# Six of eight input-weight pieces of a selective-scan layer made inside the attention before it, and the layer's opening steps interleaved

## The reference, cut to what matters

```python
proj = einsum('bld,pd->blp', hidden, in_proj_w)
gate, hbc, dt = proj[..., :I], proj[..., I:I+CONV_DIM], proj[..., -H:]
conv = conv_bias + sum_k pad(hbc)[:, k:k+L, :] * conv_weight[:, k]     # K = 4
x, B, C = split(silu(conv))
dt_p = softplus(dt + dt_bias);  A = -exp(A_log);  dA = exp(dt_p * A)
state = state * dA_t + (dt_p * x)_t * B_t;  y_t = state . C_t          # scan over tokens
y = rmsnorm_per_group(y + x * D) * norm_weight * silu(gate)
out = einsum('bli,di->bld', y, out_proj_w)
```

## Time and profile before

| | us |
|---|---|
| median of 3 runs | 4329.69 (4328.75 to 4337.84) |
| the profiled execution, its own time | 4338.59 |
| span of the profile | 4336.8 |
| PE busy | 3790.7 (87%) |
| DVE busy | 2798.5 (65%) |
| ACT busy | 2281.6 (53%) |
| POOL busy | 1887.1 (44%) |
| mean granted TensorE clock | 0.924 |

### The profile page before, as it was taken

The page is one execution under the profiler, slowest core; times in us unless marked ns, Lnnn a source line. Parts: engine busy times, 40 slices in busy tenths (PEclk is TensorE's granted clock), DMA queues, the critical chain, the costliest instruction groups (busy, mean ns, idle before and its releaser), DMA issues.

```text
span 4336.8 us, 63426 instructions
## 1 busy us (share of the span) xinstructions
PE 3790.7 (87%) x21648; PEld 1878.8 (43%) x21648; DVE 2798.5 (65%) x4529; ACT 2281.6 (53%) x3945; POOL 1887.1 (44%) x1566
## 2 busy tenths in 40 slices
PE   6799996889889858999999999999999984867899
PEld 2344442322332225555555555555555552443344
DVE  6522223675567357888888888888888866566322
ACT  5422222455445537667666766667666753453222
POOL 5400000000000217778787877778787774553000
PEclk7699996889888979999999999999999997898999
DMA  3100002000100010000000000000000001012100
GB/s 109 46 1 0 0 0 50 16 1 16 18 1 1 1 57 12 19 17 7 30 1 25 12 24 13 19 18 7 30 1 24 6 25 37 23 45 62 40 10 19
DMA packets 62763, 91.20 MB, mean 21 GB/s; under 512 B 12310, under 2 KB 36393, under 8 KB 62453
## 3 DMA queue, kind: packets, MB, share of 16 engines
q1 hardware_dynamic: 62456, 87.31, 7.2%
HBM read 73.62 MB, written 6.85 MB: 19 GB/s over the span
## 4 chain that ended last, share of the span: by engine, by line
PE 65%; DVE 15%; issue 8%; ACT 6%; POOL 3%; DMA 2%; SPq 1%; DVEq 0%; POOLq 0%; ACTq 0%
PE psum L332 14%; PE psum L333 14%; PE psum L334 14%; PE psum L1373 3%; DVE arena L1522 3%; PE psum L2434 2%; PE psum L2430 2%; PE psum L2422 2%; PE psum L1346 2%; PE psum L2391 2%; PE psum L1357 2%; PE psum L2413 1%; ACT xn L218 1%; PE psum L1342 1%; DVE x L2119 1%
## 5 line engine op out<-in xcount | busy, mean ns | idle before, releaser
L332 PE MATMUL psum<-xt_hi,arena 128*128 128x512 f16 (+1 forms) x2272 | 875.9, 386 | 48.4 <-DVE arena L1512 14.5
L333 PE MATMUL psum<-xt_lo,arena 128*128 128x512 f16 (+1 forms) x2272 | 874.3, 385 | 0.0
L334 PE MATMUL psum<-xt_hi,arena 128*128 128x512 f16 (+1 forms) x2272 | 871.9, 384 | 0.0
L2217 POOL TENSOR_TENSOR arena<-arena 128x1024 f16<-128x1024 f16 x256 | 514.3, 2028 | 79.8 <-DVE arena L2029 48.4
L1291 POOL TENSOR_TENSOR rs<-sd,epsc 128x1 f32<-128x1 f32 x15 | 8.2, 550 | 1153.5 <-DVE sd L1566 1153.5
L1522 DVE TENSOR_REDUCE arena<-psum 128x1 f32<-128x512 f32 (+3 forms) x608 | 365.1, 655 | 176.3 <-PE psum L1346 174.9
L332 PE MATMUL psum<-arena 128*128 128x512 f16 (+1 forms) x1152 | 422.2, 370 | 59.4 <-DVE arena L2842 20.5
L1474 ACT ACTIVATE arena<-psum 128x512 f32<-128x512 f32 x576 | 319.9, 598 | 276.9 <-PE psum L1357 181.4
L333 PE MATMUL psum<-arena 128*128 128x512 f16 (+1 forms) x1152 | 422.2, 370 | 0.0
L334 PE MATMUL psum<-arena 128*128 128x512 f16 (+1 forms) x1152 | 421.7, 370 | 0.0
L332 PEld LDWEIGHTS psum<-xt_hi,arena 128*128 128x128 f16 x2272 | 225.1, 99 | 301.0 <-issue 18.6
(11 more groups left out here) (330 smaller groups left out, 7834.7 us busy)
## 6 DMA issues: line engine op xcount, KB each, us to landing
arena<-m_wi SPq DMA_DIRECT2D x64, 320.0 KB, 3.0
arena<-m_wo SPq DMA_DIRECT2D x32, 256.0 KB, 2.6
arena<-arena SPq DMA_DIRECT2D x96, 64.0 KB, 2.5
x<-L_attn_x SPq DMA_DIRECT2D x4, 1024.0 KB, 8.8
out<-x SPq DMA_DIRECT2D x4, 1024.0 KB, 4.3
arena<-gate_wT SPq DMA_DIRECT2D x16, 224.0 KB, 2.6
arena<-up_wT SPq DMA_DIRECT2D x16, 224.0 KB, 2.5
arena<-down_wT SPq DMA_DIRECT2D x14, 256.0 KB, 2.6
```

The source lines that it names most:

```text
L332: nc.tensor.matmul(out, lh, rh, start=start, stop=False)
L333: nc.tensor.matmul(out, lh, rl, start=False, stop=False)
L334: return nc.tensor.matmul(out, ll, rh, start=False, stop=stop)
L2217: nc.gpsimd.tensor_tensor(m4_ar[:, q], heads[q].broadcast_to([P, HG, P]), m4_le.unsqueeze(1).broadcast_to([P, HG, P]), ALU.mult).then_inc( ...
```

## The change

Six of the eight pieces move into L1 attention: at the first unit of p = 10 to 15, ACT and DVE each make one, and SP fetches it at row p (a "piece" step each). The pieces are taken in the order 1, 2, 3, 5, 6, 7, and all six pass through the first half of m4_raw; 0 and 4, whose target overlaps L1's masks, are made after feed-forward steps 13 and 14, and the dt weights after step 15. SP fetches those two and the small parameters once the attention's last transposes are done, not after the feed-forward. L1's feed-forward weights move to other addresses, are fetched at row 11 and not 2, and split at p = 13 and not 5.

In the opening of L2 attention the 8 KB memset of m4_acc shrinks to its last tile; group 0 writes m4_acc by `tensor_scalar` instead of adding to it. Both dt products run at once, in two banks (7 and 3). The projections 0 to 3, their `before` and their convolutions are laid between the links of the two step-size chains; 4 to 9 follow. ACT waits for x_kept ahead of the first Abs.

```diff
@@ steps2
-                    if p == 5 and i == 0:
+                    if p == 13 and i == 0:
                         steps.append(("ffn_weights", 0))
+                    if p >= EARLY4 and i == 0:
+                        steps.append(("piece", p - EARLY4))
...
                 steps.append(("ffn", n))
+                if n in (LAST3 + 1, LAST3 + 2):
+                    steps.append(("piece", NT - EARLY4 + n - LAST3 - 1))
+                if n == LAST3 + 3:
+                    steps.append(("dt_weights", 0))
...
+        EARLY4 = NT - 6
@@ sp_l1_attn
                 elif what == "row":
-                    if p == 2:
+                    if p >= EARLY4:
+                        if p > EARLY4:
+                            sp.wait_ge(m4_wlo, p - EARLY4 + 2)
+                        sp_piece(sp, p - EARLY4)
+                    if p == 11:
+                        sp.wait_ge(a2_md, AT2["qp", 1, 1, KT - 1] + 3)
+                        sp.wait_ge(a2_dma, 16 * 2 * QDMA)
                         sp.dma_start(s3_raw, ...).then_inc(s3_in, 16)
@@ sp_l2_attn
+        FIRST4 = (1, 2, 3, 5, 6, 7, 0, 4)
...
-            arena_free(sp, 4)
+            sp.wait_ge(a2_at, 2 * NT)
+            sp.wait_ge(m4_wlo, 6 + 2)
+            for i in (6, 7):
+                sp_piece(sp, i)
...
-            for q in range(2):
-                fetch(q, wi, q, SW)
...
-            for q in range(2, QI):
-                sp.wait_ge(m4_wlo, q + 1)
-                fetch(q, wi, q, SW)
@@ new
+        def act_first_piece(act, i):
+            q = FIRST4[i]
+            act.wait_ge(m4_ri[i // 7], 16 if i == 7 else 16 * (i + 1))
+            nc.scalar.activation(m4_wh[:, q % KT, ...], m4_raw[:, i // 7, :], ACT.Copy,
+                                 scale=WS).then_inc(m4_whi, 1)
+        def dve_first_piece(dve, i):
...
+            dve.wait_ge(m4_whi, i + 1)
...
@@ act_l2_attn
-            act.wait_ge(m4_cin, 6 * 16)
-            nc.scalar.activation(m4_na, m4_na, ACT.Exp).then_inc(m4_dw, 1)
-            nc.scalar.activation(m4_dh, m4_dr, ACT.Copy, scale=WS).then_inc(m4_dw, 1)
-            for j in range(QI):
-                act_piece(act, 0, j)
+            act.wait_ge(x_kept, 16)
             for n in range(2):
...
                 nc.scalar.activation(m4_v, m4_v, ACT.Ln, bias=1.0).then_inc(m4_ta, 1)
+                before(act, 0, 0, 2 * n)
                 act.wait_ge(m4_tv, 4 * n + 2)
...
                 nc.scalar.activation(m4_ah[:, hc], m4_u, ACT.Copy).then_inc(m4_ta, 1)
+                before(act, 0, 0, 2 * n + 1)
                 act.wait_ge(m4_dp, n + 3)
                 nc.scalar.activation(m4_v, psum[:, 6, :], ACT.Exp).then_inc(m4_ta, 1)
-                act.wait_ge(m4_tv, 4 * n + 4)
-            act.wait_ge(x_kept, 16)
-            for q in range(CT):
+            for q in range(4, CT):
                 before(act, 0, 0, q)
@@ dve_l2_attn
-            nc.vector.memset(m4_acc, 0.0)
+            nc.vector.memset(m4_acc[:, CG - 1, :], 0.0)
...
-            for j in range(QI):
-                dve_piece(dve, 0, j)
+            conv_params(dve, 0)
+            skip_params(dve, 0)
...
                 nc.vector.tensor_scalar(m4_u, m4_u, -1000.0, None, ALU.max).then_inc(m4_tv, 1)
+                convolve(dve, ch, 0, 0, 2 * n)
                 dve.wait_ge(m4_ta, 5 * n + 4)
                 nc.vector.tensor_tensor(m4_al[:, hc], ...).then_inc(m4_tv, 1)
+                convolve(dve, ch, 0, 0, 2 * n + 1)
...
-            for i in range(CT):
+            for i in range(4, CT):
                 convolve(dve, ch, 0, 0, i)
@@ add_out
+            if isinstance(gi, int) and gi == 0:
+                nc.vector.tensor_scalar(acc, psum[:, OB[j % 4], :], m4_rs, None, ALU.mult).then_inc(m4_ok, 1)
+                return
@@ pe_l2_attn
             for n in range(2):
-                if n:
-                    pe.wait_ge(m4_tv, 4 * n - 3)
...
             for n in range(2):
                 hc = slice(n * 8 * HS, (n + 1) * 8 * HS)
+                in_proj(pe, 0, 0, 2 * n)
+                in_proj(pe, 0, 0, 2 * n + 1)
                 pe.wait_ge(m4_tv, 4 * n + 3)
...
+            for q in range(4, FT):
+                in_proj(pe, 0, 0, q)
             pe.wait_ge(m4_ta, 10)
             pe.wait_ge(m4_tv, 8)
-            for q in range(FT):
-                in_proj(pe, 0, 0, q)
```

More of the change, by code:

```diff
@@ L778, in build @@
         UNIT2 = paired2()
[L781 to L784, removed]
+        s3_raw = carve(98816, [KT, C], F32)
+        s3_h = carve(81920, [KT, C], F16)
+        s3_l = carve(86016, [KT, C], F16)
+        s3_s = carve(90112, [8], F32)
         s3_in = sem("s3_in")
@@ L1496, in act_l1_attn @@
                     act_l1_weights(act)
+                elif what == "piece":
+                    act_first_piece(act, p)
+                elif what == "dt_weights":
+                    act_dt_weights(act)
                 elif what == "ffn":
@@ L1593, in dve_l1_attn @@
                     dve_l1_weights(dve)
+                elif what == "piece":
+                    dve_first_piece(dve, p)
+                elif what == "dt_weights":
+                    dve_dt_weights(dve)
                 elif what == "ffn":
@@ L1805, in act_piece @@
         def act_piece(act, gi, j):
-            act.wait_ge(m4_ri[j % 2], (gi * (QS // 2) + (j // 2 + 1)) * 16)
+            act.wait_ge(m4_ri[j % 2], (gi * (QS // 2) + (j // 2 + (1 - 3 if j % 2 else 1 + 3))) * 16)
             q = j % QS
@@ L1825, in dve_piece, with act_dt_weights, dve_dt_weights @@
                                            op0=ALU.mult, op1=ALU.subtract).then_inc(m4_wlo, 1)
+        def act_first_piece(act, i):
+            q = FIRST4[i]
+            act.wait_ge(m4_ri[i // 7], 16 if i == 7 else 16 * (i + 1))
+            nc.scalar.activation(m4_wh[:, q % KT, q // KT * SW:(q // KT + 1) * SW], m4_raw[:, i // 7, :], ACT.Copy,
+                                 scale=WS).then_inc(m4_whi, 1)
+        def dve_first_piece(dve, i):
+            q = FIRST4[i]
+            if i == 0:
+                dve.sem_inc(m4_wlo, 2)
+            dve.wait_ge(m4_whi, i + 1)
+            w = slice(q // KT * SW, (q // KT + 1) * SW)
+            nc.vector.scalar_tensor_tensor(out=m4_wl[:, q % KT, w], in0=m4_raw[:, i // 7, :], scalar=WS,
+                                           in1=m4_wh[:, q % KT, w], op0=ALU.mult, op1=ALU.subtract).then_inc(m4_wlo, 1)
+        def act_dt_weights(act):
+            act.wait_ge(m4_cin, 6 * 16)
+            nc.scalar.activation(m4_na, m4_na, ACT.Exp).then_inc(m4_dw, 1)
+            nc.scalar.activation(m4_dh, m4_dr, ACT.Copy, scale=WS).then_inc(m4_dw, 1)
+        def dve_dt_weights(dve):
+            dve.wait_ge(m4_cin, 6 * 16)
+            dve.wait_ge(m4_dw, 2)
+            nc.vector.scalar_tensor_tensor(out=m4_dl, in0=m4_dr, scalar=WS, in1=m4_dh, op0=ALU.mult,
+                                           op1=ALU.subtract).then_inc(m4_dw, 1)
         def act_l2_attn(act):
@@ L2016, in dve_l2_attn @@
                 dve.wait_ge(m4_dp, n + 1)
-                nc.vector.scalar_tensor_tensor(out=by_tile(m4_u), in0=by_tile(ps_m), scalar=1.0 / WS,
+                if n:
+                    dve.wait_ge(m4_tv, 4)
+                nc.vector.scalar_tensor_tensor(out=by_tile(m4_u), in0=by_tile(psum[:, 7 - 4 * n, :]), scalar=1.0 / WS,
                                                in1=m4_db.unsqueeze(1).broadcast_to([P, 8, HS]), op0=ALU.mult,
@@ L2032, in dve_l2_attn @@
             dve.wait_ge(m4_tv, 8)
-            conv_params(dve, 0)
-            skip_params(dve, 0)
-            for i in range(CT):
+            for i in range(4, CT):
                 convolve(dve, ch, 0, 0, i)
@@ L2280, in pe_l2_attn @@
                     for k in range(KT):
-                        last = three(pe, ps_m[:, j * HS:(j + 1) * HS], xt_hi[:, k, tok], xt_lo[:, k, tok],
+                        last = three(pe, psum[:, 7 - 4 * n, j * HS:(j + 1) * HS], xt_hi[:, k, tok], xt_lo[:, k, tok],
                                      m4_dh[:, k, :], m4_dl[:, k, :], k == 0, k == KT - 1)
@@ L2355, in in_proj @@
             if x == 0 and q == 0:
-                pe.wait_ge(m4_wlo, gi * QS + (KT + 2))
+                pe.wait_ge(m4_wlo, gi * QS + ((QI if isinstance(gi, int) and gi == 0 else KT) + 2))
             if x == 0 and q == 5:
```

8 lines of the change are left out of this document (3 added, 5 removed).

## The result

| | before | after |
|---|---|---|
| median, us (lowest to highest, runs) | 4333.8 (4328.8 to 4349.7, 8) | 4315.0 (4309.3 to 4321.9, 8) |
| profiled execution (its span) | 4338.6 (4336.8) | 4315.6 (4313.8) |
| ratio, 95% interval | | 0.996 (0.9943 to 0.9976) |

The change gains 18.8 us; 20.7 were predicted. I cut this stretch at three marks: SP's first row of maxima (735.03 before, 735.56 after), DVE's statistics of step 13 (1522.62, 1526.45) and the start of the last xt_lo (1550.68, 1558.50).

The account below looks back on a forecast made before the run. The opening of L2 attention was taken as the bound, with PE waiting on memset, pieces and step-size chains. Terms: -29.7 opening + 5 L1 attention + 4 feed-forward = -20.7 us, from median 4329.7 to 4309.0; range 4297 to 4320.

Parts of the forecast that it names:

- What bounds the kernel, and the opening: L2 attention's opening: PE waits behind memset, pieces and two step-size chains; new order gains 28.8 us, 29.7 with P0.
- al behind a convolution: Opening, DVE: half 0's al waits behind convolution 0 until 14.2 us after P0 and ends at 14.9.
- Table load: Opening, ACT: `before`'s Identity directly behind an Ln needs no table load of its own, cost 0; otherwise 1.28 us twice.
- Projection 0 at 10.4: Opening: projection 0 is ready 10.4 us after P0, so `before` 0 runs from 10.4 to 11.7.
- The tail, 4: Feed-forward: pieces behind steps 13 and 14 delay DVE's statistics by 2.0 and 1.9 us; cost 4, between 2 and 5.5.
- The memset's "cover": Opening, DVE: short memset and conv_params, 2 to 4 us, lie beside PE's 5.1 us dt product; uncovered, half 0 loses 1.
- L1 attention, 5: L1 attention, p = 10 to 15: six pieces stop DVE and ACT and cost 5 us, between 0 and 8.5.
- between -2 and 2: L1 attention: moving the split from p = 5 to 13 meets the same density and costs 0 us.
- (c): Rival, L1 attention: each stop also drops the clock, 4.0 us each, 24 for six; 4328, no change; chance 0.10.
- (a): Rival: pieces and split hide in L1 attention, and the clock holds for projection 4; -28, or 4301; chance 0.22.
- (b): Rival: opening gains less, by half clock for projections 0 and 1 or longer al wait; -16, or 4314; chance 0.08.
- (d): Rival, L1 attention: each piece holds DVE's and ACT's queues like the split, 6.8 us each; +15, or 4345; chance 0.04.

Follow-up runs that it names:

- e3: After, with the opening back in the old order (pieces stay moved, memset short); opening 43.0 us, run once: 4328.4 us.
- e4: After, with pieces, dt weights and split back in their old places (opening interleaved, memset short); opening 48.3 us, run once: 4318.4 us.
- e11: After, with only the store of x issued as soon as its ten tiles are final; opening 33.9 us, run once: 4329.0 us.
- e5: After, with both tail pieces moved behind feed-forward step 15, next to the dt weights; tail 28.2 us, run once: 4322.2 us.
- e2: After, with the whole memset of m4_acc put back; opening 35.3 us, run once: 4321.1 us.
- e1: Before, with only the split of L1's feed-forward weights moved from p = 5 to 13; run once: 4329.4 us.
- e6: After, with DVE's al ahead of convolution 2n, and half 0's dt2 and half 1's u ahead of convolution 1; opening 32.2 us, once: 4301.8 us.
- e7: After, with all six L1 attention pieces in the last query tile, p = 15; run once: 4307.2 us.
- e8: After, with the edits of e5, e6 and e7 together; 4306.6 us (5 runs), ratio to before 0.9932.
- e9: e8, with the six pieces earlier in the last tile, ahead of the first feed-forward steps; 4302.5 us (6 runs), ratio to before 0.9925.
- e10: e9, with the store of x issued as soon as its ten tiles are final; 4301.6 us (6 runs), ratio to before 0.9932.

## Why the prediction was right, and where it was not

**What bounds the kernel, and the opening: right.** The path was memset, pieces and step sizes in a row: e3 and e4 give 8.3 and 13.6 to the two parts, each taken last. Of the terms, ACT's hold on x_kept, Ln, and al behind a convolution came within 0.1 us, and the clock's fall before projection 4 came as said. Table load: none behind Ln, neither ahead of L1982 nor of its Identity, L1983 (1583.35), so the 0 stands. The load for Ln takes from Exp's end at 1581.02 to 1582.34. That is 1.3 us, and the Trainium skill's 2.66 with a drain (ScalarE: Activation LUTs, What ACT_TABLE_LOAD costs) is not seen here either. "Projection 0 at 10.4" was wrong by 2.2 us: the sum looked at the store of x only for who waits on its semaphore, not for what else uses the DMA engines, and took the dt product's half clock from before, 1 us too short; in e11, with the store gone, projection 0 was read at 11.1 behind P0. It cost the gain 1.1 in the end (-28.6 for -29.7), because projection 4 took 4.6 and not 5.0, and some slack took up the rest.

**The tail, 4: right,** term by term, and e5 shows the cause: the wait of an in-order DVE for ACT's half.

**The memset's "cover":** the short memset and conv_params were done 1.4 us behind P0, so this held; the whole memset would not have been covered (e2: 1.3 us on the chain). Its worth was on the path before.

**L1 attention, 5: near for the pieces, wrong for the split.** By stage (us; the idle time also up to p = 10 and from there on; the split is at p = 5 in before and e4, at 13 in all others):

| kernel | pieces at | stage | PE busy | idle | up to p = 10 | from p = 10 | clock |
|---|---|---|---|---|---|---|---|
| before / e1 / e4 | in the opening | 787.6 / 778.4 / 787.8 | 691.7 / 685.1 / 691.9 | 95.9 / 93.3 / 95.9 | 50.7 / 45.8 / 50.7 | 45.2 / 47.5 / 45.2 | .88 / .89 / .88 |
| after / e2 / e3 | p = 10 to 15 | 790.9 / 797.4 / 797.4 | 694.6 / 701.0 / 703.7 | 96.3 / 96.5 / 93.7 | 44.4 / 44.8 / 44.5 | 51.9 / 51.7 / 49.2 | .87 / .87 / .86 |
| e5 / e6 / e11 | p = 10 to 15 | 804.9 / 783.7 / 804.7 | 709.4 / 686.3 / 708.5 | 95.5 / 97.4 / 96.2 | 45.5 / 45.2 / 45.6 | 49.9 / 52.2 / 50.6 | .86 / .89 / .86 |
| e7 / e8 | p = 15 | 787.3 / 790.8 | 690.3 / 697.8 | 97.1 / 93.0 | 45.5 / 45.2 | 51.6 / 47.8 | .88 / .87 |
| e9 / e10 | p = 15 | 783.7 / 787.0 | 690.8 / 694.6 | 93.0 / 92.4 | 44.6 / 44.3 | 48.3 / 48.1 | .88 / .87 |

The idle time of the whole stage is 95.9 before and 95.9 in the mean of the six kernels with the pieces at p = 10 to 15, as if they were free. In two parts it looks otherwise. From p = 10 on the six have 50.9 in the mean, and e1, with the same split and no piece, 47.5: six pieces cost about 3.4 us, and about 1.5 at p = 15 (49.0 in the mean of four). My 5, from "a stop comes through nearly whole", was 1.6 too high but right in kind. The step that failed is the 0, "between -2 and 2", for moving the split from p = 5 to 13: up to p = 10 the stage has 50.7 us of idle time with the split at p = 5 and 44.3 to 45.8 without it, and from there on the split adds 2.3, so that moving it gained about 3 (2.6 in e1). PE's stop at it is the same in both places, 4.32 and 4.33; why the parts around it differ stays open. All this rests on one kernel, e1, and on a scatter of 3 to 4 between kernels of the same steps in the second part, so 3.4 and 3 are good to some 2 us.

The measured +3.3 is then 0.4 of idle time, pieces against split, and 2.9 of PE's longer busy time at a lower clock. So my sum met the profiled pair (-20.7 on both sides) partly by luck: 4.6 us too much idle time stood against the 2.9, 0.5 from ahead of the stage and 1.1 from the opening.

**Rivals.** (c), a clock that drops at each stop for 24 us in all, did not happen in the profile of after; the stages between 783.7 and 804.9 us of one and the same step list are the nearest thing to it. Much of that is not the pieces' doing: up to p = 10, where none stands, the eleven kernels with the split at 13 already took 441.5 to 453.3 us, at clocks of 0.88 to 0.85. From p = 10 on, PE was busy 289.4 us in each of the three kernels without pieces, 288.0 to 301.7 in the six with them at p = 10 to 15, and 282.6 to 299.4 in the four with them at p = 15. Whether the pieces make low-clock stretches likelier is not settled by so few, and with it the clock's share in the 8.4 us between e8 and after stays open. (a) has the clock at projection 4 wrong (0.50, not full), and its cheap stage came true in the sum of idle time alone, not because the pieces hide. (b) is out by the opening: projections 0 and 1 ran at full clock, and it gained 28.6, not 25. (d) is out: the interval ends at 0.9976.

## What to carry to other kernels

A wait of one engine is filled for nothing by work whose own waits end inside it: the same two pieces cost 4 us at steps 13 and 14 and nothing behind step 15. Where the clock makes a stage longer or shorter by several us, judge moved work by idle time and not by length; and where an edit moves two things, part the stage between them, or the gain of one hides the cost of the other, as 3 us of the split hid 3.4 of the pieces here. And where an engine stands for "issue" beside a large DMA, ask whether that DMA can go earlier, even where nobody's semaphore hurries for it.

## What the runs showed of the hardware that I had not expected

**The clock of one stage differs from run to run.** From the first row of maxima to step 13, six kernels with the same steps took 783.7 to 804.9 us, at mean granted clocks of 0.89 to 0.86, with idle times within 3.7 us of one another. The tail, by contrast, is 28.1 or 28.2 us in all kernels without its two pieces and 31.9 to 32.1 in those with them.

**A store can hold PE.** 1.30, 1.79 and 3.00 us of "issue" ahead of projection 0 in after, e8 and e9, and 1.6 to 1.7 in e2, e5, e6 and e7, none in e10 and e11 with the 2.56 MB store moved away. In all seven PE went on 3.1 to 3.7 us behind the store's landing.

**DVE slows beside POOL.** Convolution 3 took 5.35 us, where convolutions 0 to 2 took 2.33, while POOL worked at its first spread (in before and e3, where POOL stands during it, convolution 3 took 2.33 as well):

```profile
1587.92 4.51 POOL L2263 TENSOR_TENSOR arena<-arena 128x1024 f16<-128x1024 f16 x2 [33.75 <-DVE arena L2074]
```

Nothing up to the read of projection 4 waited for it. The Trainium skill (GPSIMD Engine Reference, Specifications) says that GpSimd shares its SBUF interfaces with VectorE, with contention for instructions with two SBUF inputs. A convolution step has two, and this row agrees.
